# Graph attention kernel on one core: the edge stage's hand-overs between engines are set one step further apart, with a second buffer where one was shared

## The reference

```python
h = jnp.maximum(_layernorm(x, axis=-1), 0.0)
q, k, v = linear(h, wq, bq), linear(h, wk, bk), linear(h, wv, bv)
scores = jnp.sum(q[dst] * k[src], axis=-1) * scale
scores = scores + (edge_weight[:, None] @ we + be)[:, 0]
seg_max = jax.ops.segment_max(scores, dst, num_segments=n)
exp_s = jnp.exp(scores - seg_max[dst])
denom = jax.ops.segment_sum(exp_s, dst, num_segments=n)
attn = exp_s / jnp.maximum(denom[dst], 1e-12)
out = jax.ops.segment_sum(v[src] * attn[:, None], dst, num_segments=n)
y = layer_norm(h + out + linear(h, ws, bs), g1, b1)
return x + layer_norm(y + linear(gelu(linear(y, w_ff1, b_ff1)), w_ff2, b_ff2), g2, b2)
```

## Time and profile before

| | |
|---|---|
| Median of three runs | 3200.69 us (3179.23 to 3219.67) |
| Profiled execution, first to last instruction | 3211.3 us; no other time is given for it |
| PE / PEld / DVE / ACT / POOL busy | 76% / 62% / 55% / 37% / 51% |
| Mean granted TensorE clock | 0.921 |
| Edge stage | about 143 to 2949 us |

### The profile page before, as it was taken

The page is one execution under the profiler, slowest core; times in us unless marked ns, Lnnn a source line. Parts: engine busy times, 40 slices in busy tenths (PEclk is TensorE's granted clock), DMA queues, the critical chain, the costliest instruction groups (busy, mean ns, idle before and its releaser), DMA issues. The chain is left out here.

```text
span 3211.3 us, 68474 instructions
## 1 busy us (share of the span) xinstructions
PE 2427.3 (76%) x14747; PEld 1996.1 (62%) x14748; DVE 1767.6 (55%) x7372; ACT 1193.2 (37%) x2930; POOL 1635.5 (51%) x1828
## 2 busy tenths in 40 slices
PE   7577677777777777777777777777777777778998
PEld 5455556556555556565656566665666666657897
DVE  7454455555555545554555555555555555556787
ACT  6333333333333333333333333333333333334666
POOL 5355565555555545555554555555555445441154
PEclk8898899899899989998998999899988899999999
DMA  7233333333233323333233333332333233222222
GB/s 231 76 103 103 99 105 101 103 98 107 90 100 100 96 86 101 97 98 96 90 102 92 96 90 96 96 98 87 96 96 100 87 92 95 83 93 71 82 74 68
DMA packets 148148, 311.29 MB, mean 97 GB/s; under 512 B 33566, under 2 KB 84625, under 8 KB 148104
## 3 DMA queue, kind: packets, MB, share of 16 engines
q0 software_dynamic: 75264, 205.62, 21.5%
q1 hardware_dynamic: 54718, 90.19, 8.6%
q10 hardware_dynamic: 18122, 14.96, 1.5%
HBM read 290.21 MB, written 20.43 MB: 97 GB/s over the span
## 5 line engine op out<-in xcount | busy, mean ns | idle before, releaser
L488 POOL DMA_INDIRECT work<-h_rows,idx x1536 | 1457.3, 949 | 1339.9 <-SPq L372 956.2
L1079 PE MATMUL bank<-work 128*128 x3520 | 939.0, 412 | 24.5 <-issue 17.7
L1011 PE MATMUL bank<-q,onehot 128*128 x5304 | 804.6, 291 | 1.2 <-DVE work L832 0.7
L1079 PEld LDWEIGHTS bank<-work 128*128 128x128 f32 x3520 | 700.1, 211 | 146.8 <-issue 45.2
L886 DVE CUSTOM_DVE_ANT_0 work<-bank,work 128x512 f32<-128x512 f32 x440 | 330.5, 751 | 778.7 <-remote 476.4
L622 ACT COPY work<-bank 128x256 f32<-128x256 f32 x880 | 295.0, 376 | 1182.6 <-remote 812.8
L832 DVE SCALAR_TENSOR_TENSOR work<-bank,work 128x257 bf16<-128x257 f32 x1764 | 651.6, 425 | 143.5 <-PE bank L1011 44.2
L1017 PE MATMUL bank<-ident,work 128*128 128x128 f32 x1764 | 307.4, 302 | 500.5 <-ACT work L622 313.3
L1011 PEld LDWEIGHTS bank<-q,onehot 128*128 128x128 bf16 x5304 | 549.5, 104 | 85.4 <-issue 1.7
L1017 PEld LDWEIGHTS bank<-ident,work 128*128 128x128 f32 x1764 | 212.8, 148 | 578.0 <-ACT work L622 442.4
L1066 PE MATMUL bank<-ident,work 128*128 128x128 f32 x1760 | 283.6, 285 | 191.8 <-ACT work L619 182.8
(11 more groups left out here) (195 smaller groups left out, 1519.5 us busy)
## 6 DMA issues: line engine op xcount, KB each, us to landing
dst_words<-dst_short SPq DMA_DIRECT2D x99, 512.0 KB
work<-h_rows,idx POOLq DMA_INDIRECT x1568
bias<-h_rows ACTq DMA_DIRECT2D x56, 128.0 KB
r_rows<-bias ACTq DMA_DIRECT2D x55, 128.0 KB
work<-r_rows SPq DMA_DIRECT2D x49, 128.0 KB, 2.3
h_rows<-acc SPq DMA_DIRECT2D x12, 512.0 KB, 6.6
work<-in_x SPq DMA_DIRECT2D x12, 512.0 KB, 3.5
out<-work SPq DMA_DIRECT2D x48, 128.0 KB, 1.7
```

Of the source, the lines that this page charges most:

```text
L488: pool.indirect_dma_start(rows[:, u, j, 0:D], None, h_rows, bass.IndirectOffsetOnAxis(idx[:, half, u * J + j:u * J + j + 1], 0)).then_inc( ...
L1011: last = nc.tensor.matmul(banks[j][:, 0:D1], onehot[:, k, j, :], q3[:, bass.ds(b, 1), c, 0:D1], start=(c == 0), stop=(c == 2))
L1079: last = nc.tensor.matmul(banks[6 + k][:, 0:D1], probs[:, j, :], rows[:, bass.ds(slot, 1), j, :], start=(j == 2), stop=(j == 1))
```

## The change

- **Step words** are packed as block * 32768 + chunk instead of chunk * 64 + block; `block_of`, `chunk_of`, `slot_of` and `place_of_mark` take them apart with one operation each or so. `not_below_zero` masks a loaded count before it is bounded.
- **Buffers.** `masked` (and so `probsT`) gets two halves, `probs` two tiles, `product` four, `decay` four columns. Some small tiles move into `mean` and `norms`.
- **Banks.** Bank 4 holds spread scores alone and bank 5 all four turned groups. The turn moves out of bank 5 into columns 258 to 385 of banks 6 and 7, in two halves at different steps.
- **Order.** In step `s` PE spreads step `s + 1`, then multiplies the second half of the sums of step `s - 1`, turns the probabilities of `s`, expands `q` for `s + 3`, and finishes the sums of `s - 1`. DVE makes the scores of `s + 2` and adds the sums of `s - 2`. ACT prepares the mask ahead of the copy of the turned probabilities, which is one instruction over 512 columns.
- **New waits.** In steps `u` = 2, 3, 5 and 6 of a trip DVE waits, ahead of `add_sums`, until ACT has copied a half of the turn out of bank 6 or 7 (`hTe_copied`, `r_copied`).
- One product of zeros stands ahead of the first sums; two sums are added behind the loop. `free_tab` counts one step more before a slot is free.

```diff
-        masked = part(C)
+        masked = part(2 * C).rearrange("p (k n) -> p k n", k=2)
         probsT = masked
-        probs = part(C).rearrange("p (j n) -> p j n", j=J)
-        product = part(J * (D1 + 1) // 2, BF16).rearrange("p (j n) -> p j n", j=J)
+        probs_even = part(C).rearrange("p (j n) -> p j n", j=J)
+        products = [part((D1 + 1) // 2, BF16)] + [norms[:, k * (D1 + 1) // 2:(k + 1) * (D1 + 1) // 2].bitcast(BF16) for k in range(J - 1)]
         assert used[0] <= PLAN_FIRST
         used[0] = PLAN_FIRST
...
+        probs_odd = part(C).rearrange("p (j n) -> p j n", j=J)
+        probs = [probs_even, probs_odd]
...
+        decay = small(4)
+        R_AT = D1 + 1
...
         def block_of(eng, step):
-            return eng.snap(eng.to_reg(step & (BLOCKS - 1)), min_val=0, max_val=B)
+            return eng.snap(eng.to_reg(step >> CHUNK_BITS), min_val=0, max_val=B)
 
         def chunk_of(eng, step):
-            return eng.snap(eng.to_reg(step >> (BLOCKS.bit_length() - 1)), min_val=0, max_val=B * TP + U)
-
-        def slot_of(eng, chunk):
-            return eng.snap(eng.to_reg(chunk & (S - 1)), min_val=0, max_val=S - 1)
+            return eng.snap(eng.to_reg(step & (CHUNKS - 1)), min_val=0, max_val=CHUNKS - 1)
+
+        def slot_of(eng, step):
+            return eng.snap(eng.to_reg(step & (S - 1)), min_val=0, max_val=S - 1)
...
-                nc.scalar.activation(decay[:, 1:2], eps[:, 0:1], ACT.Exp, scale=0.0).then_inc(sums_set, 1)
+                nc.scalar.activation(decay[:, 2:3], eps[:, 0:1], ACT.Exp, scale=0.0)
+                nc.scalar.activation(decay[:, 3:4], eps[:, 0:1], ACT.Exp, scale=0.0).then_inc(sums_set, 1)
...
+                def copy_hTe(turn, c):
+
+                    act.wait_ge(hTe_ready, turn * 2 + (c + 1))
+                    nc.scalar.copy(hT_e[:, c * P:(c + 1) * P], banks[6 + c][:, R_AT:R_AT + P]).then_inc(hTe_copied, 1)
+                    if c == DC - 1:
+                        act.dma_start(h_in, h_rows[bass.ds((turn + 1) % B * P, P), :]).then_inc(h_back, 16)
+
+                def copy_r(turn, n):
+
+                    if n == 1:
+                        act.wait_ge(r_stored, turn * 16 + 16)
+                    act.wait_ge(r_ready, turn * 2 + (2 - n))
+                    nc.scalar.copy(r_out[:, n * P:(n + 1) * P], banks[6 + n][:, R_AT:R_AT + P]).then_inc(r_copied, 1)
...
                     for u in range(steps):
                         s, k = first + u, u % 2
                         act.wait_ge(masked_done, s + 1)
-                        nc.scalar.activation(decay[:, k:k + 1], old_max[:, k:k + 1], ACT.Exp, bias=new_max, scale=-1.0)
-                        nc.scalar.activation(probsT, masked, ACT.Exp, bias=new_max, scale=-1.0).then_inc(exp_done, 1)
-                        for half in (1, 0):
-                            act.wait_ge(turned, s * 2 + (2 - half))
-                            nc.scalar.copy(probs[:, 2 * half:2 * half + 2, :].rearrange("p j n -> p (j n)"), banks[5 - half][:, 0:2 * P]).then_inc(probs_done, 1)
+                        nc.scalar.activation(decay[:, u % 4:u % 4 + 1], old_max[:, k:k + 1], ACT.Exp, bias=new_max, scale=-1.0)
+                        nc.scalar.activation(probsT[:, k, :], masked[:, k, :], ACT.Exp, bias=new_max, scale=-1.0).then_inc(exp_done, 1)
                         prepare(s + 2, k)
-                        for at, body in ((3, copy_hTe), (6, copy_r), (7, store_r)):
-                            if steps == U and u == at:
-                                body(act.snap(act.to_reg(r * NW + i), min_val=0, max_val=B * NW))
+                        act.wait_ge(turned, s + 1)
+                        nc.scalar.copy(probs[k][:].rearrange("p j n -> p (j n)"), banks[5][:]).then_inc(probs_done, 1)
+                        if steps == U and u in (2, 3):
+                            copy_hTe(act.snap(act.to_reg(r * NW + i), min_val=0, max_val=B * NW), u - 2)
+                        if steps == U and u in (5, 6):
+                            copy_r(act.snap(act.to_reg(r * NW + i), min_val=0, max_val=B * NW), 6 - u)
+                        if steps == U and u == 7:
+                            store_r(act.snap(act.to_reg(r * NW + i), min_val=0, max_val=B * NW))
...
                         dve.wait_ge(spread, step)
                         dve.wait_ge(outside_done, step)
                         dve.wait_ge(max_read, step)
-                        nc.vector.tensor_tensor_reduce(out=masked, in0=banks[4][:], in1=outside[:, k, :], scale=-1.0, scalar=old_max[:, k:k + 1],
+                        nc.vector.tensor_tensor_reduce(out=masked[:, k, :], in0=banks[4][:], in1=outside[:, k, :], scale=-1.0, scalar=old_max[:, k:k + 1],
                                                        op0=ALU.add, op1=ALU.min, accum_out=new_max).then_inc(masked_done, 1)
-                        edge_scores(step_at(regs[u + 1]), r, s + 1, 1 - k, meanwhile)
+                        edge_scores(step_at(regs[u + 2]), r, s + 2, k, meanwhile)
...
+                        blocks[u + 4] = place[0][2]
+                        dve.wait_ge(outside_done, prepared)
+                        mark(place[0], k)
                         read_max(s + 1, 1 - k, block_at(u + 1))
-                        add_sums(s, 1 - k, dve.snap(held, min_val=0, max_val=B) if u == 0 else blocks[u - 1])
-                    dve.reg_mov(held, dve.to_reg(blocks[steps - 1]))
+                        if steps == U and u in (2, 3):
+                            dve.wait_ge(hTe_copied, dve.to_reg((r * NW + i) * 2 + (u - 1)))
+                        if steps == U and u in (5, 6):
+                            dve.wait_ge(r_copied, dve.to_reg((r * NW + i) * 2 + (u - 2)))
+                        add_sums(s, u + 2, dve.snap(held[u], min_val=0, max_val=B) if u < 2 else blocks[u - 2])
...
+                def turn_probs(k):
+
+                    for j in range(J):
+                        last = nc.tensor.transpose(banks[5][:, j * P:(j + 1) * P], probsT[:, k, j * P:(j + 1) * P], ident[:])
+                    last.then_inc(turned, 1)
+
+                def sum_rows(k, half, slot):
+
+                    for j in (2 * half, 2 * half + 1):
+                        last = nc.tensor.matmul(banks[6 + k][:, 0:D1], probs[k][:, j, :], rows[:, bass.ds(slot, 1), j, :], start=(j == 2), stop=(j == 1))
+                    if half == 0:
+                        last.then_inc(summed, 1)
...
+                pe.wait_ge(dotted, 2)
+                expand_q(1, 1, ahead[1])
                 pe.wait_ge(scored, 1)
                 spread_scores(0)
-                pe.wait_ge(dotted, 2)
-                expand_q(1, 1, ahead[1])
+                pe.wait_ge(onehot_done, S + 3)
+                pe.wait_ge(dotted, 3)
+                expand_q(0, 0, ahead[2])
+                pe.wait_ge(dotted, 4)
+                expand_q(0, 1, ahead[2])
...
-                        b, slot = block_of(pe, step_of[u + 2]), slot_of(pe, step_of[u] >> (BLOCKS.bit_length() - 1))
+                        b = block_of(pe, step_of[u + 3])
+                        pe.wait_ge(masked_done, s + 1)
+                        pe.wait_ge(scored, s + 2)
+                        spread_scores(1 - k)
+                        pe.wait_ge(probs_done, s + 1)
+                        sum_rows(1 - k, 1, slot)
                         pe.wait_ge(exp_done, s + 1)
-                        for half in (1, 0):
-                            for j in range(2):
-                                last = nc.tensor.transpose(banks[5 - half][:, j * P:(j + 1) * P], probsT[:, (2 * half + j) * P:(2 * half + j + 1) * P], ident[:])
-                            last.then_inc(turned, 1)
-                        pe.wait_ge(onehot_done, s + (S + 3))
-                        pe.wait_ge(dotted, s * 2 + 3)
-                        expand_q(k, 0, b)
-                        pe.wait_ge(scored, s + 2)
-                        pe.wait_ge(probs_done, s * 2 + 1)
-                        spread_scores(1 - k)
-                        pe.wait_ge(dotted, s * 2 + 4)
-                        expand_q(k, 1, b)
-                        for j in (2, 3, 0, 1):
-                            if j == 0:
-                                pe.wait_ge(probs_done, s * 2 + 2)
-                            last = nc.tensor.matmul(banks[6 + k][:, 0:D1], probs[:, j, :], rows[:, bass.ds(slot, 1), j, :], start=(j == 2), stop=(j == 1))
-                        last.then_inc(summed, 1)
-                        if steps == U and u == 2:
-                            turn_h(pe.snap(pe.to_reg(r * NW + i), min_val=0, max_val=B * NW))
-                        if steps == U and u == 5:
-                            project_h(pe.snap(pe.to_reg(r * NW + i), min_val=0, max_val=B * NW))
+                        turn_probs(k)
+                        pe.wait_ge(onehot_done, s + (S + 4))
+                        pe.wait_ge(dotted, s * 2 + 5)
+                        expand_q(1 - k, 0, b)
+                        pe.wait_ge(dotted, s * 2 + 6)
```

(9 more changed lines are left out.)

163 lines of the change are left out of this document (91 added, 72 removed).

## The result

The changed kernel takes 3221.07 us (3200.34 to 3241.03, 20 runs) beside 3208.10 us of before (3179.23 to 3230.84, 20 runs): 1.0047 of it, 95% interval 1.0027 to 1.0068. No change by the 2% that count here, where 2950 us (2700 to 3190) was forecast. The profiled execution spans 3212.2 us, before 3211.3.

The account below looks back on a forecast made before the run. The prediction took PE's results, held late during POOL's gather bursts, to bound the kernel at about one step a cycle. From 3200.7 us it took 253 and added about 2 for the ends: 2950 us (2700 to 3190).

Parts of the forecast that it names:

- The hold: Edge stage: PE's results reach other engines late from about 2 us into a gather burst until 2 us after its last start.
- each of the 384 chunks ... costs one short cycle: Edge stage: each chunk gathered in the loop takes one one-chunk burst cycle, 384 x 6.53 = 2508 us.
- absorbed: Edge stage: the 48 steps that take no new chunk, and late starts, add no time.
- The 253 us: Edge stage: forecast saving from the slack, 2551 us against 2804 us, chosen between ends of 0 and 480.
- the best case: Edge stage: two-chunk bursts passing two full steps, 5.94 us a chunk, 2324 us in all, 480 less.
- DVE's new waits: Four steps of eight: add_sums waits behind ACT's turn copy, 0.4 to 0.55 us more each; nothing without gathers.
- the 108 us: Worst cost of DVE waiting for turn copies, 196 x 0.55 us, taken to cancel against two-chunk bursts passing more steps.
- Sums one step later: POOL's slots and DVE's sums: later sums still leave gathered rows four chunks ahead; costed at nothing.
- The forecast of about 700: POOL's gather: its wait on SP (L488) should fall from 956 us to about 700 as a sign of being right.
- The lock stays: Rival, edge stage: still one step a cycle, sums only at a release, nothing moves; 3150 to 3220 us, chance 0.16.
- No hold at all: Rival, edge stage: waits are only the chain's own, gathers delay nothing; 2370 us, chance 0.07.

Follow-up runs that it names:

- before_words: The kernel before with only the step words repacked chunk low and loaded counts masked: 2333.32 us, 0.9997 of the kernel before.
- after_shift_third: Third timing of the changed kernel with 80 fillers moving DVE's loop, where the kernel before takes 3258.41 us: 3199.87 us, 0.9804 of it.
- after_nogather: The changed kernel with 80 fillers moving DVE's loop, without 384 of 392 gathered chunks: 2299.98 us, 0.9858 of the kernel before.
- after_shift: The changed kernel plus 80 semaphore increments in DVE's queue that only move its loop's code: 2371.74 us, 1.0162 of the kernel before.
- after_shift_copyfirst: after_shift with ACT's copies of the turn ahead of its wait for the turned probabilities: 2350.58 us, 1.0072 of the kernel before.
- after_again: The changed kernel itself, unaltered, timed again where the kernel before takes 2334.87 us: 2620.22 us, 1.1227 of it.

## Why the prediction was wrong

**The hold: right in the job that it was read from.** In held jobs PE's results are late while POOL gathers in long bursts, and leaving out gathers gives 1000 us back. The reading from two windows stands for the whole stage. In the changed kernel 137 of 440 copies start more than 1.5 us behind the start of their transposes, up to 8.27 us, and 111 of these 137 start 2 to 3 us after the last gather of a burst has started. But the hold isn't a property of the kernel: four jobs in six don't show it. It reaches ahead of the loop, too. In the stretch from 80 to 100 us, in which POOL gathers the first 32 groups of rows, PE (first number behind the length) is busy 3.80 us in before and 17.12 us in `before_words`, a free job:

```profile
80.00:100.00 20.00, 3.80 (x14) 2.36 (x12) 6.78 (x24) 0.97 (x4) 15.19 (x16) 0.59 0.35 102
```

```profile
80.00:100.00 20.00, 17.12 (x96) 13.54 (x94) 16.41 (x49) 12.30 (x41) 15.17 (x16) 1.00 0.59 155
```

Even the first mask comes at 143.6 us there and at 114.0 us here. What makes a job held I don't know; the chip doesn't, since two chips gave both. Nor do the traces tell whether PE finishes late or the news of it travels late, since the ends of matmuls are modelled.

**The step that failed: "each of the 384 chunks ... costs one short cycle" of 6.53 us, with all else "absorbed".** The 253 us are nothing but this step, and the recorded rows already spoke against it. With 319 waits of POOL for 440 steps the old order passed 1.38 steps a cycle, not one. At most 65 chunks started without a wait, which can put 130 of 384 chunks into bursts of two, so the short cycle wasn't "by far the commoner" by chunks. And of the three releases in the earlier trace rows the prediction used the two of 1.82 and 1.93 us and left out the third, 3.54 us, behind the burst of two.

Counted over the whole stage (masks from 1 us behind a burst's start to 1 us behind the next one's), the old order had 320 bursts, 1.37 masks in a cycle of one chunk and 1.39 in one of two. A short cycle took 7.24 us on average, not 6.53. The changed kernel has 297 bursts: 1.25 masks in the 195 short cycles and 1.92 in the 91 long ones (67 before). So the slack works, but in the long bursts, where the 253 us had no term, and it makes these commoner. And neither cycle is as short as was costed: a chunk of the changed kernel costs 7.53 us in a short cycle and 13.63 / 2 = 6.82 in a long one, where the sum had 6.53 and the best case 5.94.

What was to be absorbed is POOL's pauses. Beyond the 0.30 us that lie between any two gathers they add up to 840 us before (53 of them longer than 4 us, 356 us together), 829 now and 808 in `after_shift_third`; the gathers make 1922 us in each. The slack is worth 11 to 32 us of pauses between these traces, and with the gaps gone 2% of the time (58 us) in a held job, against 253.

**The term that was missing: code loading.** The sum held nothing for the place of DVE's loop, although the change makes it 14 instructions longer and starts it 32 records later. It costs 248 us in a free job, the largest part of the 12% there, and by the estimate above about 78 us in a held one. By that estimate it is what turned a 2% gain into the null result: without it the changed kernel would take about 0.9804 x 3208 = 3145 us, inside the outer range but still 195 us above the forecast. So both steps failed, and the 253 us by more.

**DVE's new waits: the mechanism right, its reach too small.** The addition's idle time rises from 230.4 to 591.6 us, in steps 2, 3, 5 and 6 as said. But the wait was to cost nothing without gathers, and it costs 77 us there (1915.0 us from the first mask to the last in `after_nogather`, 1837.7 with the copies first) and 21 us with gathers in a free job (`after_shift` against `after_shift_copyfirst`), since it stands behind ACT's 512-column copy there as well. That the 108 us would cancel against something else had no row behind it.

**Sums one step later: nothing, as said.** SP's wait in POOL's rows went from 956.2 to 948.3 us. DVE's wait for landed rows is 22.0 us there. The forecast of about 700 for the first was the same wrong step as the 253.

**The rivals.** "The lock stays" (3150 to 3220 us) named the outcome within 1 us, by luck: its reason was one step a cycle, and the masks did pair up. "No hold at all" came to 2370 us by POOL's 5.03 us a chunk, and `after_shift` takes 2371.74 in a free job. Its floor for POOL was right (1932 us costed, 1931 measured); that the total agrees within 2 us is partly luck, since the stage took longer than the floor (1986 us from the first mask to the last) and the ends took less. There the rule of the Trainium skill (SBUF — State Buffer, "Who interferes with whom") is borne out (no copy over 1.10 us behind its transposes), while in held jobs results are late all the same, up to 8.27 us. But before takes 2334 us there, so even that rival was no gain, but 1.6% slower.

## What to carry to other kernels

When an engine runs a loop of some hundred instructions, look at the gap behind its jump and at the packets of the instruction queue before and after a change: an edit that only adds or moves a few instructions can put 3 us behind every trip, on top of what PE's lower clock behind each pause takes, and fillers ahead of the loop take it away again. Before paying for slack in a chain, count what the pacing engine (here POOL's 1536 gathers) needs by itself, and count cycles, steps per cycle and the length of a pause over the whole stage, not in one window. And time the kernel before in more than one job: a bound that a single trace shows may belong to the job.

## What the runs showed of the hardware

- Results of PE reach other engines late during bursts of four and more gathers by POOL in some jobs (1.84 to 3.93 us from the transposes to the copy in the rows shown, up to 8.27 us in `after`) and not in others (0.47 us in the rows shown, never over 1.10 us in `after_shift`), at the same 0.95 us for one gather. With bursts of two hardly any does (1920 us from the first mask to the last against 1914). What makes a job one or the other is open.
- POOL starts an indirect gather of 128 rows every 1.25 us, 1536 in a row; small additions between them use most of the 0.30 us in between.
- A loop of 332 or 335 instructions on DVE jumps back in 0.23 to 0.31 us or in 2.99 to 3.63 us, by its place alone.
- PE's granted clock falls from 1.00 to 0.50 in a pause of 4 us behind such a jump and is back at 1.00 some 11 us behind it (`after_again`).
